# Edge-maximum passes of a four-layer graph network: the gathered rows are transposed into PSUM as first member of the sum, and the edges of the next group are made between the product and the turned scan

## The reference, cut to what matters

```python
def _edge_conv(x, src, dst, W1, b1, W2, b2, n_nodes):
    xi = x[dst]
    xj = x[src]
    m = jnp.concatenate([xi, xj - xi], axis=-1)
    h = jax.nn.relu(m @ W1 + b1) @ W2 + b2
    agg = jax.ops.segment_max(h, dst, num_segments=n_nodes)
    return jnp.where(jnp.isfinite(agg), agg, 0.0)
```

## Time and profile before

| | |
|---|---|
| median of three runs | 14293.22 us |
| the profiled execution: time, span | 14320.16 us, 14318.4 us |
| its mean granted clock of TensorE, as a share of 2.4 GHz | 0.737 |
| busy over the span: TensorE, weight loads | 8175.9 us (57%), 6995.2 us (49%) |
| VectorE, ScalarE, GpSimd | 7060.5 us (49%), 2195.9 us (15%), 7386.1 us (52%) |
| gathers L1438 of the three passes | 2496, 2360.1 us busy |

### The profile page before, as it was taken

The page is one execution under the profiler, slowest core; times in us unless marked ns, Lnnn a source line. Parts: engine busy times, 40 slices in busy tenths (PEclk is TensorE's granted clock), DMA queues, the critical chain, the costliest instruction groups (busy, mean ns, idle before and its releaser), DMA issues. The chain is left out here.

```text
span 14318.4 us, 190871 instructions
## 1 busy us (share of the span) xinstructions
PE 8175.9 (57%) x43167; PEld 6995.2 (49%) x43168; DVE 7060.5 (49%) x14119; ACT 2195.9 (15%) x6082; POOL 7386.1 (52%) x7807
## 2 busy tenths in 40 slices
PE   4677344442444436666364455555577767776776
PEld 3666344442344435555243355544466656665665
DVE  4555211113333337888788455566444444444444
ACT  0000000000111110000000000034233323332332
POOL 3666577773566506777000377600266646654665
PEclk6555566665566568988788666666799989998998
DMA  2222555554222215666343244432244434443444
GB/s 72 84 85 84 140 97 97 97 96 106 63 60 59 57 20 171 204 203 198 77 135 102 75 131 130 130 88 81 72 129 129 129 97 129 129 122 103 129 129 115
DMA packets 1058180, 1558.40 MB, mean 109 GB/s; under 512 B 340400, under 2 KB 512092, under 8 KB 1058128
## 3 DMA queue, kind: packets, MB, share of 16 engines
q1 hardware_dynamic: 667296, 920.90, 22.6%
q0 software_dynamic: 329776, 470.23, 14.8%
q10 hardware_dynamic: 61056, 166.75, 3.0%
HBM read 1223.25 MB, written 333.93 MB: 109 GB/s over the span
## 5 line engine op out<-in xcount | busy, mean ns | idle before, releaser
L1438 POOL DMA_INDIRECT T<-gather_d,srci x2496 | 2360.1, 946 | 2563.6 <-PEq L70 1119.2
L1069 PE MATMUL PS<-T 128*128 x3392 | 1132.2, 426 | 1045.8 <-DMA T<-wide_d,slot_idx 340.2
L1551 DVE TENSOR_TENSOR_SCAN T<-T,PS 128x512 f32<-128x512 f32 x624 | 798.7, 1280 | 1798.3 <-PE PS L1480 1746.9
L732 POOL DMA_INDIRECT added_d<-T,slot_idx x840 | 1305.5, 1554 | 364.3 <-issue 194.5
L1069 PEld LDWEIGHTS PS<-T 128*128 128x128 f32 x3392 | 769.2, 259 | 1231.3 <-issue 1174.9
L1480 PE MATMUL PS<-T,W 128*128 128x512 f32 x1248 | 749.6, 684 | 982.5 <-issue 836.7
L1244 PE MATMUL PS<-T 128*128 128x260 f32 (+1 forms) x3360 | 870.1, 421 | 518.2 <-DVE T L1293 316.5
L1031 POOL DMA_INDIRECT T<-wide_d,slot_idx x848 | 940.9, 1110 | 378.4 <-issue 254.5
L1070 PE MATMUL PS<-T,ident 128*128 128x256 f32 (+1 forms) x3392 | 1072.0, 408 | 0.0
L504 POOL DMA_INDIRECT T<-score_d,slot_idx x848 | 856.5, 1010 | 373.6 <-issue 312.1
L1466 PE MATMUL PS<-T 128*128 128x128 f32 x4992 | 1009.2, 285 | 68.7 <-DMA T<-gather_d,srci 64.4
(11 more groups left out here) (249 smaller groups left out, 16224.6 us busy)
## 6 DMA issues: line engine op xcount, KB each, us to landing
T<-onehot_t_d SPq DMA_DIRECT2D x1258, 256.0 KB
T<-step_first_d SPq DMA_DIRECT2D x624, 256.0 KB
edge_rows_d<-T ACTq DMA_DIRECT2D x212, 512.0 KB
T<-step_src_d SPq DMA_DIRECT2D x422, 256.0 KB
T<-edge_rows_d SPq DMA_DIRECT2D x210, 512.0 KB
onehot_t_d<-T SPq DMA_DIRECT2D x212, 256.0 KB
edge_rows_d<-T ACTq DMA_DIRECT2D x212, 256.0 KB
T<-edge_rows_d SPq DMA_DIRECT2D x210, 256.0 KB
```

Of the source, the lines that this page charges most:

```text
L732: gp.indirect_dma_start(added_d[k][:, :], bass.IndirectOffsetOnAxis(ap=slot_idx[:, k:k + 1], axis=0), quad(OUT8, g)[:, u * P:(u + 1) * P], ...
L1069: T_.matmul(spot(g, u), part(quad(OT8, g), u), T2[:, bass.ds(bs[4 * g + u] * width, width)], start=True, stop=False)
L1438: gp.indirect_dma_start(part(R[n % RING], u), None, gather_d[:, :], bass.IndirectOffsetOnAxis(ap=srci[:, k:k + 1], axis=0)).then_inc(rows_ ...
L1551: V.tensor_tensor_scan(SC[i], MK[r], bank(2 + i), SC[1 - i][:, GROUP * P - 1:GROUP * P], ALU.add, ALU.max).then_inc(scanned.h, 1)
```

## The change

The two matmuls of `make_edges` change places, and the one with the identity becomes a transposition (`is_transpose=True`), which now opens the sum in PSUM; the matmul with OT is added to it. The edges run a group ahead of the rest: TensorE makes edges(0) ahead of the loop and then, for each group, products(n), edges(n+1), turn(n), ends(n-1). ScalarE's order becomes relu(n+1), lay(n+2), turn_out(n), with two lays and a relu ahead of the loop. VectorE's becomes scan(n), mark_ends(n), add(n-1). So that the loop needn't end in a special case, a group past the last one is gathered, its one-hots are loaded, and its edges are made.

```diff
@@ -1431,7 +1431,7 @@
                 def _(gp):
-                    for n in range(GROUPS):
+                    for n in range(GROUPS + 1):
                         gp.wait_ge(edges_made.h, edges_made.done(n - RING))
@@ -1440,22 +1440,25 @@
                 def _(sp):
+                    def hots(n, j, r):
+                        sp.wait_ge(edges_made.h, edges_made.done(n - RING))
+                        sp.dma_start(OT[r], onehot_t_d[:, bass.ds(j * (per_trip * P) + (r * GROUP + LEAD) * P, GROUP * P)]).then_inc(hots_in[r].h, 16)
+
                     with sp.Fori(0, trips) as j:
...
                             s0 = j * per_trip + (r * GROUP + LEAD)
-                            sp.wait_ge(edges_made.h, edges_made.done(n - RING))
-                            sp.dma_start(OT[r], onehot_t_d[:, bass.ds(j * (per_trip * P) + (r * GROUP + LEAD) * P, GROUP * P)]).then_inc(hots_in[r].h, 16)
+                            hots(n, j, r)
                             sp.wait_ge(scanned.h, scanned.done(n - RING))
...
                             sp.dma_start(MK[r], row.to_broadcast([P, GROUP * P])).then_inc(firsts_in[r].h, 16)
+                    hots(GROUPS, trips, 0)
 
...
                 def _(pe):
-                    for s in (edges_made, products_made):
+                    for s in (edges_made, products_made, turned):
                         s.lead(pe)
-                    for s in (turned, ends_made):
-                        s.lead(pe, 1)
+                    ends_made.lead(pe, 1)
 
@@ -1463,8 +1466,8 @@
                         for u in range(GROUP):
-                            T_.matmul(part(bank(r % 2), u), part(AB[r % 2], u), part(OT[r], u), start=True, stop=False)
-                            last = T_.matmul(part(bank(r % 2), u), part(R[r], u), ident[:, :], start=False, stop=True)
+                            T_.matmul(part(bank(r % 2), u), part(R[r], u), ident[:, :], start=True, stop=False, is_transpose=True)
+                            last = T_.matmul(part(bank(r % 2), u), part(AB[r % 2], u), part(OT[r], u), start=False, stop=True)
                         last.then_inc(edges_made.h, 1)
@@ -1487,21 +1490,21 @@
 
+                    make_edges(0, 0, 0)
                     with pe.Fori(0, trips) as j:
...
                             n = j * RING + r
-                            make_edges(n, j, r)
-                            turn(n - 1, 1 - r % 2)
                             make_products(n, r % 2)
+                            make_edges(n + 1, j + (r + 1) // RING, (r + 1) % RING)
+                            turn(n, r % 2)
                             make_ends(n - 1, 1 - r % 2)
-                    turn(GROUPS - 1, 1)
                     make_ends(GROUPS - 1, 1)
...
                         s.lead(act)
-                    turned_out.lead(act, 1)
+                    turned_out.lead(act)
 
@@ -1519,16 +1522,18 @@
 
-                    lay(0, 0, numbers_at(act, brow, LEAD, GROUP, BLOCKS))
+                    first = numbers_at(act, brow, LEAD, 2 * GROUP, BLOCKS)
+                    lay(0, 0, first[0:GROUP])
+                    lay(1, 1, first[GROUP:])
+                    relu(0, 0)
                     with act.Fori(0, trips) as j:
...
                             if r % 2 == 0:
-                                bs = numbers_at(act, brow, j * per_trip + (r * GROUP + LEAD + GROUP), 2 * GROUP, BLOCKS)
-                            relu(n, r % 2)
-                            turn_out(n - 1, 1 - r % 2)
-                            lay(n + 1, 1 - r % 2, bs[r % 2 * GROUP:r % 2 * GROUP + GROUP])
-                    turn_out(GROUPS - 1, 1)
+                                bs = numbers_at(act, brow, j * per_trip + ((r + 2) * GROUP + LEAD), 2 * GROUP, BLOCKS)
+                            relu(n + 1, 1 - r % 2)
+                            lay(n + 2, r % 2, bs[r % 2 * GROUP:r % 2 * GROUP + GROUP])
+                            turn_out(n, r % 2)
 
@@ -1568,16 +1573,18 @@
                             scan(n, j, r)
+                            mark_ends(n, r % 2, j * per_trip + (r * GROUP + LEAD))
                             add(n - 1, 1 - r % 2, bs[r % 2 * GROUP:r % 2 * GROUP + GROUP])
-                            mark_ends(n, r % 2, j * per_trip + (r * GROUP + LEAD))
                     c.close(trips)
                     add(GROUPS - 1, 1, numbers_at(dve, brow, LEAD + (GROUPS - 1) * GROUP, GROUP, BLOCKS))
-            for s in (edges_made, products_made, relued, scanned, end_hots, turned, ends_made, turned_out, added):
+            for s in (products_made, scanned, end_hots, turned, ends_made, turned_out, added):
                 s.passed(GROUPS + RING)
-            laid.passed(GROUPS + 1 + RING)
+            for s in (edges_made, relued):
+                s.passed(GROUPS + 1 + RING)
+            laid.passed(GROUPS + 2 + RING)
             for r in range(RING):
-                rows_in[r].passed(64 * trips)
-                hots_in[r].passed(16 * trips)
+                rows_in[r].passed(64 * (trips + (r == 0)))
+                hots_in[r].passed(16 * (trips + (r == 0)))
                 firsts_in[r].passed(16 * trips)
```

## The result

| | before | after |
|---|---|---|
| median of four runs each, same chip | 14298.0 us (14289.47 to 14307.19) | 14371.07 us (14364.6 to 14401.35) |
| the profiled execution: time, span | 14320.16, 14318.4 us | 14364.6, 14362.8 us |
| first gather of the passes to the end of the span | 10209.9 to 14318.4: 4108.5 us | 10176.8 to 14362.8: 4186.0 us |

The ratio is 1.0055, with an interval of 1.0038 to 1.0073. Faster by 1.2% was forecast. The passes alone are 77.5 us longer. Groups per pass are as before; the windows, in the columns of the earlier trace rows, hold 707 gathers where 720 were, and a lower granted clock.

A forecast was written before the change was run, and what follows sets the result against it. The bound was a cycle of four gathers worked off at 1.43 us each before the edges' report is seen. 14320 - 189 (longer bursts) + 15 (extra group) - 27 (profiled run above median) gave 14,120 us, range 14,070 to 14,211.

The forecast's parts named there:

- the line: Burst of gathers to release of TensorE's reports: 1.43 us per gather plus 0.14 us once, fitted to bursts of 4 and 20.
- the hold: What TensorE finishes during a burst of gathers is seen by other engines only once the burst is worked off; mechanism unnamed.
- Step (a): Transposition in the edges: four instructions for eight a group, 0.44 us off TensorE, worth nothing alone inside 2 us of idle.
- Step (b): TensorE's new order: next group's edges from T+1.62, last start T+2.84, seen about T+3.15; without gathers about 3.6 us a loop.
- T: Moment a group's edges are reported made, when relu, the next one-hot load and the next gather start.
- Step (c): Edges seen at T+3.15, before the fourth gather, lengthen GpSimd's bursts: 5.80 us a group, 0.31 us less, 189 us in all.
- merged bursts: GpSimd running on into the next group without pause: 8 gathers or more, two groups in 11.7 us, 5.86 us a group.
- Step (d): ScalarE and VectorE orders: a held turn may delay relu, but so is everything; idle time in 5.8 us covers their work.
- Step (f): Group past the end replaces a tail group, a lay and 1.3 us of edges: about 5 us a pass, 15 in all.
- R3: Rival, TensorE's clock: granted clock below 0.8, half the groups at 1.2 GHz cost 290 us; 14,600 us, chance 0.20.
- R2: Rival, nothing moves: T stays 6.0 to 6.11 us and only 15 us are added; 14,300 us, chance 0.17.
- R1: Rival, no hold left: GpSimd's issue sets 5.0 us a group; 13,650 us, chance 0.20.

## Why the prediction was wrong

- **The bound** was named rightly: a cycle of one burst worked off at 1.43 us a gather. The experiment without gathers hit its time (13,300 expected, 13,298.65), and bursts of 8 and 20 obey the line (11.8 us against 11.6; 11583.37 to 11611.79 = 28.4 us against 28.7). But it says of the hold "what TensorE finishes during a burst of gathers", and that is too wide: it is the edges' report and what is finished behind it.
- **Step (a), the transposition, "on its own worth nothing"**: it takes 0.44 us from TensorE as said (tail groups 4.03 us for 4.49), but alone it is worth 0.23 to 0.27%. About 0.05 us a group comes from reports seen that much earlier; the mechanism isn't known.
- **Step (b)** was exact: the last edge starts at T+2.83.
- **Step (c) is the one that failed: "edges seen at T+3.15 are seen before the fourth gather and before the hold".** They are made at T+2.83 and seen at T+6.0. The premise was that the hold doesn't begin at once, read from the end sums of the slow group, which came through at T+3.7. They did, and so did the end sums of all 609 steady groups of before, made 2.2 to 3.9 us behind the first gather. But they are finished ahead of the edges. The edges' report itself, made 3.9 to 4.2 us behind the first gather, was held in all 501 groups of before that have it there, and made at 2.6 us it is held as well. So what came through was another kind of report, and its early place in the burst, which the prediction took as the reason, isn't what decided. The 189 us had no other support.
- **The merged bursts** that did come (38) were to be worth 0.25 us a group each. They come from the few reports seen early, not from a report ahead of the hold. The drain of the one shown is as computed, but the order behind it loses more: the turn stands before the products, which the prediction took as "what is late next", with a whole period to spare. It has that in a burst of four, not behind one of eight.
- **Step (d), "relu is late, but so is everything"**: true until the report comes; after it add, scan, turn, end sums and products run one behind the other, 5.2 us, and that isn't shared with anything.
- **Step (f)**: about 5 us in all and not 15.
- **Sums**: the loop without gathers adds up to 3.62 us in step (b), and R3 uses 3.53; by the same terms the work without the turn falls from 3.63 to 2.74 us a group, not from 3.5 to 2.6. Neither moves the forecast.
- **R2** comes nearest, T stays 6.04, but it had only 14,300. **R3** had the right sign, but its mechanism isn't what happened: the clock fell to 0.91, not below 0.8, and the order alone is slower with the clock at 0.95. Behind a merged burst 1.2 GHz lengthens the chain (end sums 1.91 us for 1.06), which is a part of its cost. **R1's** pace of 5.0 us is what the whole change has, but on chips without a hold, where the kernel before has 5.1 already.

## What to carry to other kernels

A result made earlier is worth nothing where its report is held by something else. Before pricing an earlier instruction, sort the trace's reports by kind and see which come through: here the end sums did and the edges didn't, so a case of another kind proved nothing. Two edits that are each small needn't add: test each alone before both. A loop order is to be judged also from the state behind a stall, where every queue's head waits: behind a merged burst three groups took 18.2 us in the old order and 21.1 in the new one.

## What the runs showed of the hardware

- On three chips (the first one, A and B) TensorE's report of the edges, and what it finishes behind them, is seen late while GpSimd gathers (up to 3.3 us for the edges), and what it finishes ahead of them isn't; on four others (C to F) nothing of this is seen (0.31 to 0.54 us in each trace). The same kernel takes 14,300 us on the former and 13,470 to 13,510 on the latter: 620 us of it in the passes (4108.5 against 13474.9 - 9985.9 = 3489.0 us) and the rest, 224 us, in earlier stages. The mechanism isn't known.
- On chips without the hold the best measured are the whole change (0.9954, 0.9957) and the transposition alone (0.9962), not told apart. With the hold it is the transposition alone (0.9973, 0.9977): it is faster on both kinds, and the change is on one only.
- A float32 transposition that opens a sum takes one issue of 0.11 us, where a matmul with the identity takes two: the twelve instructions of a group's edges in the changed kernel start 0.11 us apart, 10399.85 to 10401.07.
- TensorE's granted clock was 0.16 to 0.20 for 13 ms in one run, and the kernel took 22.1 ms.
